# One unrolled pipeline in place of three passes, and a causal mask added by TensorE instead of a minimum on VectorE

## The chip, the cores and the metric

One core of one Trainium2 chip runs the whole kernel in one launch. The metric is the device time of the kernel in microseconds (us), and less is better. Engines are named as in the profile: PE is TensorE's matmul, PEld its weight load, DVE is VectorE, ACT is ScalarE, POOL is GpSimd, SP is SyncE, which here issues every transfer.

## What is computed

Sixteen images of 3x256x256 go through an edge filter, one block of attention with a causal mask, and one linear layer with the signs of a weight. All of it is in float32, S = D = 256, 16 heads of 16.

```python
gray = einsum('bchw,c->bhw', x, (0.2989, 0.587, 0.114))
h = abs(conv3x3(gray, scharr)).sum(axis=filters) / 2          # two 3x3 filters, zero padding
c_q, c_kv = norm(h) @ W_dq, norm(h) @ W_dkv                   # 256 -> 64 each
Q, K, V = c_q @ W_uq, c_kv @ W_uk, c_kv @ W_uv                # 64 -> 16 heads x 16
scores = where(tril, Q @ K.T / 4, -inf)
h = h + softmax(scores) @ V @ W_o
out = h + norm(h) @ sign(weight).T                            # norm is a layer norm without weights
```

## The kernel before

The kernel is written engine by engine: five programs, one for each engine, that wait for each other by semaphores. An engine runs its own program strictly in the written order, and an instruction that waits holds up all that stand behind it. There are 128 partitions, so an image of 256 rows lies in T = 2 tiles.

**Front pass.** SP loads an image (`x_sb`), ACT and DVE make it gray (L557, L686, L689), SP stores it with a border to DRAM (`gray_padded`) and loads it again as overlapping bands (`rows`, five transfers). PE applies the filters as products with `band` (L824), ACT takes absolute values (L563), DVE adds the two filters into `h_all`, forms mean and variance (`bn_stats`, `bn_aggr`) and the normalised `xn`. PE transposes it (L817), compresses to 64+64 (L853) and expands to queries, keys (L845) and values (L859). To reach float32 precision with bf16 products, each of query and key is cut into three bf16 parts: ACT casts the first (L573), DVE takes the rest (L724) and casts the second (L727), POOL takes the third (L503). SP stores the parts to DRAM (`qk_parts`) and later loads them in the layout in which six products of parts are one contraction of 96 rows (`q_st`, `k_st`, twelve transfers an image).

**Attention pass.** It starts when the front pass is through. Per image there are four groups g of four heads. For group g, PE forms the scores of the second half of the queries against all keys (`ps_hi`, L876 and mask L878) and of the first half against the first keys (`ps_lo`, L890 and mask L892). DVE takes their negated maxima (L752, L756). POOL cuts the maxima of two groups into three bf16 parts (`cut_max`, L515 to L523), PE transposes them, ACT copies them, SP moves them to three more rows of `q_st`. One iteration later PE forms the transposed scores of the same image with the maximum subtracted: first key block into `ps_k0` (L906, and the mask as a product of an identity with `mask_kq`, L908), second key block into `ps_k1` (L915, no mask product). DVE applies the mask of the second block, by a minimum of `ps_k1` with `cap_kq` (L761). ACT takes the exponentials (L600, L608), PE multiplies by the values with a column of ones (L927, L930), ACT copies (L616), PE transposes (L947), DVE divides (L733, L736), SP stores the result to DRAM (`attn_scratch`).

**Tail pass.** SP loads the attention output, PE transposes it (L817) and multiplies by `w_out` (L980), DVE adds `h_all` and normalises (L778, L790), PE transposes and multiplies by the signs `w_sign` (L980), DVE adds and SP stores.

What sets the order is written by hand: in each pass each engine has a step for "image n", and steps of neighbouring images are interleaved by constant offsets. The middle of each pass is a hardware loop (`Fori`) over pairs of images, the ends are unrolled. Buffers of one pass are used again in the next (`shared`, `parts`, `xn`), and the eight PSUM banks of 2 KB are laid out anew for each.

## Time and profile before

| | |
|---|---|
| three timed runs | 499.44, 499.70 and 503.98 us, median 499.70 us |
| the profiled execution | 499.42 us by the same clock, span of the trace 497.1 us |
| busy PE, PEld | 404.2 us (81%), 301.0 us (61%) |
| busy DVE, ACT, POOL | 357.1 us (72%), 223.2 us (45%), 94.1 us (19%) |
| instructions on PE, DVE, ACT, POOL | 3780 matmuls, 655, 404, 204 |
| DMA | 82.09 MB, mean 165 GB/s; the queue's packets took 58.3% of sixteen engines' span |
| mean granted clock of TensorE | 0.935 of full speed |

Busy time is counted from the first to the last instruction (the span); 2.3 us of the execution lie around it. A busy PE is one with a matmul under way, since matmuls overlap in the pipeline: the distance from one start to the next says what one costs PE, not its own length. A float32 product of 128x256 is recorded as two matmuls. The shares are means over three passes that differ, so the rows below are taken from the middle of each pass.

### The profile page before, as it was taken

What the parts mean: (1) busy time and instruction counts of PE and PEld (TensorE: products, weight loads), DVE (VectorE), ACT (ScalarE), POOL (GpSimd) and SP (SyncE); (2) the same over time, 40 slices, a digit from 0 to 9 for tenths busy, and PEclk for the clock granted to TensorE, in tenths of its full rate; (3) what the DMA queues carried; (4) which work ended last, traced back from release to release, by engine and by line L of the source; (5) the groups of instructions that cost most, each with busy time, mean ns of one, the idle gap of its engine ahead of it and who ended that gap; (6) DMA issues with size and microseconds to landing.
All of it is one profiled execution on the core that took longest, in us unless ns stands there. A gap on an engine that the chain in (4) does not pass through costs nothing.

```text
span 497.1 us, 11506 instructions
## 1 busy us (share of the span) xinstructions
PE 404.2 (81%) x3780; PEld 301.0 (61%) x3780; DVE 357.1 (72%) x655; ACT 223.2 (45%) x404; POOL 94.1 (19%) x204
## 2 busy tenths in 40 slices
PE   0068867678759667899999999999999987999995
PEld 0034634446536454567777777777777755787874
DVE  2765988877795436678888888888888835676664
ACT  2034535344444341366566656655566663222231
POOL 8500322322241133111111111111111100000000
PEclk9986978878898895799999999999999999999999
DMA  4999999999996955444444444444444222333231
GB/s 151 236 241 253 244 248 267 264 258 259 259 276 178 228 157 157 135 134 142 137 144 145 150 146 136 137 142 139 141 142 145 72 87 65 113 98 123 88 107 63
DMA packets 80863, 82.09 MB, mean 165 GB/s; under 512 B 6890, under 2 KB 74698, under 8 KB 80842
## 3 DMA queue, kind: packets, MB, share of 16 engines
q1 hardware_dynamic: 80842, 81.81, 58.3%
q8 instruction: 12, 0.20, 0.2%
q14 instruction: 9, 0.07, 0.0%
HBM read 56.17 MB, written 25.23 MB: 164 GB/s over the span
## 4 chain that ended last, share of the span: by engine, by line
PE 49%; DMA 23%; SPq 10%; issue 7%; ACT 5%; DVE 4%; POOL 1%; ACTq 0%; DVEq 0%; POOLq 0%
DMA gray_padded<-gray 16%; PE bank L980 11%; PE bank L876 6%; PE bank L906 5%; PE bank L927 5%; PE bank L947 4%; SPq L337 3%; SPq L359 3%; PE bank L908 3%; PE bank L890 3%; PE bank L878 3%; PE bank L892 3%; PE bank L915 2%; PE bank L930 2%; PE bank L817 2%
## 5 line engine op out<-in xcount | busy, mean ns | idle before, releaser
L752 DVE TENSOR_REDUCE neg_max<-bank 128x4 f32<-128x1024 f32 x64 | 78.3, 1223 | 26.5 <-PE bank L878 26.5
L600 ACT ACTIVATE shared<-bank 128x1024 f32<-128x1024 f32 x64 | 65.6, 1025 | 70.3 <-PE bank L908 70.3
L824 PE MATMUL bank<-shared,band 128*32 128x256 f32 x512 | 44.1, 503 | 37.3 <-DMA shared<-gray_padded 37.3
L503 POOL TENSOR_TENSOR parts<-rest,parts 128x1024 bf16<-128x1024 f32 x16 | 38.5, 2404 | 133.3 <-DVE parts L727 133.3
L876 PE MATMUL bank<-k_st,q_st 96*128 96x256 bf16 x256 | 48.7, 285 | 7.5 <-DMA k_st<-qk_parts 3.3
L824 PEld LDWEIGHTS bank<-shared,band 128*32 128x32 f32 x512 | 18.8, 134 | 57.6 <-issue 46.0
L761 DVE TENSOR_TENSOR bank<-bank,cap_kq 128x512 f32<-128x512 f32 x64 | 44.2, 691 | 4.3 <-PE bank L915 4.3
L906 PE MATMUL bank<-q_st,k_st 99*128 99x256 bf16 x256 | 46.3, 274 | 0.6 <-DMA q_st<-max_rows 0.6
L927 PE MATMUL bank<-shared,v_now 128*32 128x256 f32 x512 | 42.7, 389 | 1.2 <-ACT shared L616 1.2
L756 DVE TENSOR_REDUCE neg_max<-bank 128x4 f32<-128x512 f32 x64 | 43.6, 681 | 0.0
L563 ACT ACTIVATE edge<-bank 128x512 f32<-128x512 f32 x32 | 19.1, 598 | 54.0 <-PE bank L824 53.9
L608 ACT ACTIVATE shared<-bank 128x512 f32<-128x512 f32 x64 | 38.2, 597 | 10.7 <-DVE bank L761 10.4
L878 PE MATMUL bank<-mask_qk,ident_bf 128*128 128x256 bf16 x128 | 36.5, 285 | 0.0
L515 POOL CAST max_parts<-neg_max 128x16 bf16<-128x16 f32 x32 | 6.3, 196 | 158.1 <-DVE neg_max L756 158.1
L980 PE MATMUL bank<-w_sign,xn_t 128*128 128x256 f32 x128 | 31.9, 392 | 5.1 <-ACT xn_t L623 5.1
L908 PE MATMUL bank<-mask_kq,ident_bf 128*128 128x256 bf16 x128 | 35.2, 275 | 0.0
L876 PEld LDWEIGHTS bank<-k_st,q_st 96*128 96x128 bf16 x256 | 21.7, 100 | 21.0 <-issue 12.9
L980 PE MATMUL bank<-w_out,a_t 128*128 128x256 f32 x128 | 30.4, 381 | 1.4 <-ACT a_t L627 1.4
L695 DVE TENSOR_TENSOR h_all<-edge 128x256 f32 (+1 forms) x32 | 13.8, 439 | 24.5 <-ACT edge L563 24.5
L689 DVE SCALAR_TENSOR_TENSOR gray<-shared,gray 128x512 f32<-128x512 f32 x16 | 31.0, 1938 | 0.6
L906 PEld LDWEIGHTS bank<-q_st,k_st 99*128 99x128 bf16 x256 | 24.8, 99 | 10.6 <-issue 1.0
L980 PEld LDWEIGHTS bank<-w_sign,xn_t 128*128 128x128 f32 x128 | 23.0, 189 | 11.4 <-ACT xn_t L623 8.9
(100 smaller groups left out, 794.3 us busy)
## 6 DMA issues: line engine op xcount, KB each, us to landing
shared<-in_x SPq DMA_DIRECT2D x16, 768.0 KB, 7.0
shared<-gray_padded SPq DMA_DIRECT2D x48, 256.0 KB
qk_parts<-parts SPq DMA_DIRECT2D x16, 768.0 KB, 6.6
q_st<-qk_parts SPq DMA_DIRECT2D x96, 128.0 KB, 2.6
k_st<-qk_parts SPq DMA_DIRECT2D x96, 128.0 KB, 2.7
gray_padded<-gray SPq DMA_DIRECT2D x16, 258.0 KB, 6.3
attn_scratch<-attn SPq DMA_DIRECT2D x16, 256.0 KB, 2.5
a_sb<-attn_scratch SPq DMA_DIRECT2D x16, 256.0 KB, 2.8
```

The lines of the kernel that those rows point to most:

```text
L503: pool.tensor_tensor(parts[:, done.slot, SLOTS_OF_PART[2], :, :], rest[:, :, :, :], parts[:, done.slot, SLOTS_OF_PART[1], :, :], ALU.subtr ...
L600: nc.scalar.activation(probs[:, g, :, 0:S], ps_k0, ACT.Exp, scale=SCALE).then_inc(exp0_done, 1)
L752: nc.vector.tensor_reduce(neg_max[:, 1, heads], ps_hi, AX.X, ALU.max, negate=True).then_inc(max_hi_done, 1)
L756: nc.vector.tensor_reduce(neg_max[:, 0, heads], ps_lo, AX.X, ALU.max, negate=True).then_inc(max_lo_done, 1)
L761: nc.vector.tensor_tensor(ps_k1, ps_k1, cap_kq[:, :].unsqueeze(1).to_broadcast([P, G, P]), ALU.min).then_inc(capped, 1)
L824: last = nc.tensor.matmul(ps_edge[b * RB:(b + 1) * RB, t, f, :], band[:, f, :], rows[:, here.slot, t * (P // RB) + b, :], start=True, stop ...
L876: nc.tensor.matmul(ps_hi[:, b * two + i, :], q[:, hh, P:S], k[:, hh, :], start=(i == 0), stop=False, skip_group_check=True)
L878: last = nc.tensor.matmul(ps_hi[:, b * two:(b + 1) * two, P:S], ident_bf[:, :], mask_qk[:, 0:two, :], start=False, stop=True, skip_group_c ...
L906: nc.tensor.matmul(ps_k0[:, b * two + i, :], k[:, hh, 0:P], q[:, hh, :], start=(i == 0), stop=False, skip_group_check=True)
L908: last = nc.tensor.matmul(ps_k0[:, b * two:(b + 1) * two, 0:P], ident_bf[:, :], mask_kq[:, :, :], start=False, stop=True, skip_group_check ...
L927: nc.tensor.matmul(ps_o[i * VW:(i + 1) * VW, :], v_now[:, a.slot, 0, g * G + i, :], probs[:, g, i, 0:S], start=True, stop=False, skip_grou ...
L980: last = nc.tensor.matmul(dst[:, t, :], src_t[:, c, t * P:(t + 1) * P], w[:, c, :], start=(c == 0), stop=(c == T - 1))
```

## The change

The three passes become one. Each engine's program is a single loop over i = -6 to 20, unrolled by Python, in which every stage stands once with its own offset: image i+4 is made gray, i+3 is filtered, i+2 is normalised, compressed, expanded and cut into parts, i has its maxima taken, i-1 its key scores and half of its values, i-2 the other half, i-3 the projection, i-4 the last layer. With it:

- `attn_scratch` is gone: the attention output goes from SBUF straight to its transpose (16 stores and 16 loads of 256 KB less). `h_all` and `v_all` become rings of eight and five images, and POOL's copy of the values (L535) is gone, ACT copies into the ring.
- The normalisation moves from DVE and ACT (variance, square root on ACT, reciprocal, L715 and L790) to POOL (`normalize_x`, `normalize_y`): four operations on 128x2, with a power of -0.5 for the root, and two `tensor_scalar` of 128x256 each. The cast of the second part (L727) moves from DVE to ACT (`second_part`).
- The first part and its rest are taken in two halves. The absolute values are one ACT operation of 128x1024 in place of two of 512. `expand_qk` contracts 64 rows (queries from rows 0 to 63, keys from 64 to 127) where it contracted 128 rows, half of them zeros.
- PSUM banks are shared by stages that now run side by side: banks 0 and 1 by `ps_hi`, `ps_edge`, `ps_y`, `ps_z`; bank 2 by `ps_lo`, `ps_at`; 3 and 4 by `ps_k0`, `ps_qk`; 5 by `ps_k1`, `ps_mt`, `ps_yt`; 7 by `ps_xt`, `ps_c`, `ps_v`, `ps_ot`. The waits in the functions of PE say whose reader must be through.
- The mask of the second key block is one more product per group, identity by `mask_kq` (now four heads wide), added into `ps_k1`. The minimum L761 and its semaphore `capped` are gone, ACT waits for `k1_done`.

The core of the diff; the functions not shown hold the same operations as before, with the new waits:

```diff
+            for i in range(-4, LAST + 1):
+                if live(i + 1):
+                    store_parts(i + 1)
+                if live(i - 1):
+                    load_max_rows(i - 1, 1)
+                if live(i + 4):
+                    store_gray(i + 4)
+                if live(i + 6):
+                    load_x(i + 6)
+                if live(i - 4):
+                    store_z(i - 4)
+                if live(i + 1):
+                    load_operands(i + 1, 0)
+                if live(i):
+                    load_max_rows(i, 0)
+                if live(i + 4):
+                    load_rows(i + 4)
+                if live(i + 1):
+                    load_operands(i + 1, 1)
...
+            def normalize_x(n):
+                pool.wait_ge(mv_done, T * (n + 1))
+                pool.tensor_scalar(var[:, :], mv[:, :, 1], EPS, None, ALU.add).then_inc(var_done, 1)
+                pool.wait_ge(var_done, n + 1)
+                pool.tensor_tensor(rstd[:, :], var[:, :], power[:, :], ALU.pow).then_inc(rstd_done, 1)
+                pool.wait_ge(rstd_done, n + 1)
+                pool.tensor_tensor(shift[:, :], mv[:, :, 0], rstd[:, :], ALU.mult).then_inc(shift_done, 1)
+                pool.wait_ge(shift_done, 2 * n + 1)
+                pool.tensor_scalar(shift[:, :], shift[:, :], -1.0, None, ALU.mult).then_inc(shift_done, 1)
+                pool.wait_ge(shift_done, 2 * n + 2)
+                need(pool, xt_done, n)
+                for t in range(T):
+                    pool.tensor_scalar(xn[:, t, :], h_ring[:, n % H_RING, t, :], rstd[:, t:t + 1],
+                                       shift[:, t:t + 1], ALU.mult, ALU.add).then_inc(xn_done, 1)
...
+                pool.wait_ge(part1_done, n + 1)
...
+            for i in range(FIRST, LAST + 1):
+                if live(i - 1):
+                    cut_max(i - 1, 1)
+                if live(i + 2):
+                    normalize_x(i + 2)
+                if live(i - 3):
+                    normalize_y(i - 3)
+                if live(i):
+                    cut_max(i, 0)
+                if live(i + 2):
+                    third_part(i + 2)
...
+            def second_part(n):
+                act.wait_ge(rest_done, 2 * (n + 1))
+                nc.scalar.copy(parts[:, n % 2, SLOTS_OF_PART[1], :, :], rest[:, :, :, :]).then_inc(part1_done, 1)
...
+                    exp_second(i - 1, 3)
+                if live(i + 3):
+                    both_edges(i + 3)
+                if live(i - 1):
+                    copy_o(i - 1, 1)
+                if live(i + 2):
+                    second_part(i + 2)
+                if live(i - 3):
+                    copy_yt(i - 3)
...
-
-                        dve.wait_ge(k1_done, NG * done.n + g + 1)
-                        nc.vector.tensor_tensor(ps_k1, ps_k1,
-                                                cap_kq[:, :].unsqueeze(1).to_broadcast([P, G, P]),
-                                                ALU.min).then_inc(capped, 1)
...
+            nc.vector.memset(w_v[0:DC, :], 0.0)
+            for i in range(FIRST, LAST + 1):
+                if live(i):
+                    max_hi(i, 0)
+                    max_lo(i, 0)
+                if live(i - 4):
+                    add_z(i - 4)
+                if live(i + 4):
+                    rest_of_gray(i + 4)
...
-            steps(dve, tail, 0, 1)
+                if live(i):
+                    max_hi(i, 1)
+                    max_lo(i, 1)
+                if live(i - 3):
+                    add_y(i - 3)
+                if live(i):
+                    max_hi(i, 2)
+                    max_lo(i, 2)
+                if live(i - 2):
+                    normalize(i - 2, 0)
+                if live(i + 2):
+                    rest_of_parts(i + 2)
+                if live(i):
+                    max_hi(i, 3)
+                    max_lo(i, 3)
+                if live(i + 3):
+                    sum_edges(i + 3)
+                if live(i - 2):
...
+            def expand_qk(n):
+                pe.wait_ge(c_copied, n + 1)
+                need(pe, exp0_done, NG * upto(n - 4) + (3 if live(n - 3) else 0))
+                need(pe, rest_done, 2 * n)
+                for t in range(T):
+                    for i, low in ((0, 0), (1, DC)):
+                        last = nc.tensor.matmul(ps_qk[:, i, t, :],
+                                                w_qk[low:low + DC, t, :, :].rearrange("p d h -> p (d h)"),
+                                                c_t[low:low + DC, :], start=True, stop=True)
+                        if t == T - 1:
...
+            def key_scores_second(n, g):
+                q = q_st[0:KM, n % 2, :, :]
+                k = k_st[0:KM, n % 2, :, :]
...
+                if g == 1:
+                    need(pe, mt_copied, 2 * (n + 1))
+                if g == 3:
+                    need(pe, mt_copied, 2 * (n + 1) + (1 if live(n + 1) else 0))
                 for i in range(G):
                     hh = g * G + i
-                    last = nc.tensor.matmul(ps_k1[:, i, :], k[:, hh, P:S], q[:, hh, P:S],
-                                            start=True, stop=True)
...
+            def feed_forward(n):
+                pe.wait_ge(yt_copied, n + 1)
+                need(pe, max_hi_done, NG * upto(n + 3) + (1 if live(n + 4) else 0))
+                need(pe, abs_done, upto(n + 6))
+                need(pe, y_done, upto(n))
+                product(ps_z, yn_t, w_sign, ffn_done)
...
+                if live(i):
+                    hi_scores(i, 0)
+                    lo_scores(i, 0)
+                if live(i - 1):
+                    key_scores_first(i - 1, 0)
+                    key_scores_second(i - 1, 0)
+                if live(i - 4):
+                    feed_forward(i - 4)
+                if live(i - 2):
+                    values(i - 2, 2)
+                if live(i - 3):
...
+                if live(i + 2):
+                    turn_x(i + 2)
+                if live(i):
+                    hi_scores(i, 1)
+                    lo_scores(i, 1)
+                if live(i - 1):
+                    key_scores_first(i - 1, 1)
+                if live(i + 2):
+                    compress(i + 2)
+                if live(i - 1):
+                    key_scores_second(i - 1, 1)
+                if live(i - 3):
+                    project(i - 3)
+                if live(i - 2):
+                    values(i - 2, 3)
+                if live(i):
+                    hi_scores(i, 2)
+                    lo_scores(i, 2)
+                if live(i - 1):
+                    key_scores_first(i - 1, 2)
+                if live(i - 2):
+                    turn_output(i - 2, 0)
+                if live(i - 1):
+                    key_scores_second(i - 1, 2)
+                    values(i - 1, 0)
+                if live(i + 2):
+                    expand_qk(i + 2)
+                if live(i):
+                    turn_max(i, 0)
+                if live(i):
+                    hi_scores(i, 3)
+                    lo_scores(i, 3)
+                if live(i + 2):
+                    expand_v(i + 2)
+                if live(i - 1):
+                    key_scores_first(i - 1, 3)
+                    key_scores_second(i - 1, 3)
+                if live(i + 3):
+                    filters(i + 3)
+                if live(i - 1):
+                    values(i - 1, 1)
+                if live(i - 2):
+                    turn_output(i - 2, 1)
+                if live(i - 3):
+                    turn_y(i - 3)
```

PE, the end of an iteration. Before, group 3 of the attention pass: key scores of `ps_k0` and `ps_k1`, transposes of the output (`shared` is the tile of unnormalised output there), products of probabilities and values:

```order
L906 MATMUL bank<-q_st,k_st 128x256 x2
L908 MATMUL bank<-mask_kq,ident_bf 128x2x128
L906 MATMUL bank<-q_st,k_st 128x256 x2
L908 MATMUL bank<-mask_kq,ident_bf 128x2x128
L915 MATMUL bank<-q_st,k_st 128x128 x4
L947 MATMUL bank<-ident,shared 128x128 x4
L927 MATMUL bank<-shared,v_now 32x256 x4
L930 MATMUL bank<-shared,v_now 32x128 x4
```

The same place of the changed program, from the key scores of group 3 to the last instruction of the iteration:

```order
L849 MATMUL bank<-q_st,k_st 128x256 x2
L851 MATMUL bank<-mask_kq,ident_bf 128x2x128
L849 MATMUL bank<-q_st,k_st 128x256 x2
L851 MATMUL bank<-mask_kq,ident_bf 128x2x128
L868 MATMUL bank<-q_st,k_st 128x128 x4
L870 MATMUL bank<-mask_kq,ident_bf 128x512
L766 MATMUL bank<-rows,band 32x256 x16
L880 MATMUL bank<-probs,v_ring 32x256 x4
L883 MATMUL bank<-probs,v_ring 32x128 x4
L909 MATMUL bank<-ident,o_un 128x128 x4
L746 MATMUL bank<-ident,yn 128x128 x4
```

The mask product of the second block (L870) is new, and between the key scores and the values now stand the filters of image i+3 (L766); the iteration ends with the transposes of `o_un` and `yn`.

PE, the head of an iteration. Before, the key scores of group 0 up to the values:

```order
L906 MATMUL bank<-q_st,k_st 128x256 x2
L908 MATMUL bank<-mask_kq,ident_bf 128x2x128
L906 MATMUL bank<-q_st,k_st 128x256 x2
L908 MATMUL bank<-mask_kq,ident_bf 128x2x128
L915 MATMUL bank<-q_st,k_st 128x128 x4
L940 MATMUL bank<-ident_bf,max_parts 24x128 x2
L927 MATMUL bank<-shared,v_now 32x256 x4
L930 MATMUL bank<-shared,v_now 32x128 x4
```

Changed, from the key scores of group 0 on:

```order
L849 MATMUL bank<-q_st,k_st 128x256 x2
L851 MATMUL bank<-mask_kq,ident_bf 128x2x128
L849 MATMUL bank<-q_st,k_st 128x256 x2
L851 MATMUL bank<-mask_kq,ident_bf 128x2x128
L868 MATMUL bank<-q_st,k_st 128x128 x4
L870 MATMUL bank<-mask_kq,ident_bf 128x512
L753 MATMUL bank<-w_sign,yn_t 128x256 x4
L880 MATMUL bank<-probs,v_ring 32x256 x4
L883 MATMUL bank<-probs,v_ring 32x128 x4
L746 MATMUL bank<-ident,attn 128x128 x4
L896 MATMUL bank<-ident_bf,max_parts 24x128 x2
L746 MATMUL bank<-ident,xn 128x128 x4
```

The product with the signs for image i-4 (L753), which writes the bank that `ps_hi` of this very group has filled, now stands ahead of the values, and the transposes of `attn` (i-3) and `xn` (i+2) around the transposes of the maxima.

POOL, from one cut of the maxima on. Before, in the attention pass:

```order
L515 CAST max_parts<-neg_max 128x2x8
L517 TENSOR_TENSOR max_rest<-neg_max,max_parts 128x16
L521 CAST max_parts<-max_rest 128x2x8
L523 TENSOR_TENSOR max_parts<-max_rest,max_parts 128x2x8
L515 CAST max_parts<-neg_max 128x2x8
L517 TENSOR_TENSOR max_rest<-neg_max,max_parts 128x16
L521 CAST max_parts<-max_rest 128x2x8
L523 TENSOR_TENSOR max_parts<-max_rest,max_parts 128x2x8
L535 COPY v_now<-v_all 128x16x16 x2
```

Changed, from the third part of image i+2 at the end of one iteration into the next:

```order
L457 TENSOR_TENSOR parts<-rest,parts 128x1024
L415 CAST max_parts<-neg_max 128x2x8
L417 TENSOR_TENSOR max_rest<-neg_max,max_parts 128x16
L420 CAST max_parts<-max_rest 128x2x8
L422 TENSOR_TENSOR max_parts<-max_rest,max_parts 128x2x8
L427 TENSOR_SCALAR var<-mv 128x2
L429 TENSOR_TENSOR rstd<-var,power 128x2
L431 TENSOR_TENSOR shift<-mv,rstd 128x2
L433 TENSOR_SCALAR shift<-shift 128x2
L437 TENSOR_SCALAR xn<-h_ring,rstd,shift 128x256 x2
L442 TENSOR_SCALAR var<-mv 128x2
```

Behind the third part stand the cut of the maxima and then the six operations of `normalize_x`, whose result the transposes of `xn` wait for.

## Rows read from the trace of the kernel before

**Rows 1.** Stretch of front, attention, tail: length, busy PE, PEld, DVE, ACT, POOL, PEclk, DMA, GB/s
```profile
75.58:154.23 78.65, 57.18 (x404) 39.13 (x404) 60.85 (x107) 33.45 (x61) 20.36 (x8) 0.83 0.96 256
...
230.74:387.22 156.48, 152.40 (x1922) 117.27 (x1921) 130.76 (x193) 96.22 (x169) 28.27 (x120) 1.00 0.47 143
415.00:488.00 73.00, 67.44 (x353) 56.59 (x351) 50.95 (x151) 20.54 (x46) 0.00 (x0) 1.00 0.32 101
```

**Rows 2.** Timeline of PE, one attention iteration, full clock
```profile
302.52 0.38 PE L876 MATMUL bank<-k_st,q_st 96*128 96x256 bf16 x2
...
303.41 0.38 PE L892 MATMUL bank<-mask_qk,ident_bf 128*128 128x512 bf16 x1
303.63 0.38 PE L906 MATMUL bank<-q_st,k_st 99*128 99x256 bf16 x2
...
304.52 0.61 PE L947 MATMUL bank<-ident,shared 128*128 128x128 f32 x4
305.06 0.64 PE L927 MATMUL bank<-shared,v_now 128*32 128x256 f32 x8
...
305.85 0.39 PE L876 MATMUL bank<-k_st,q_st 96*128 96x256 bf16 x2
...
315.07 0.66 PE L947 MATMUL bank<-ident,shared 128*128 128x128 f32 x4 [0.35 <-ACT max_rows L591]
315.56 0.38 PE L876 MATMUL bank<-k_st,q_st 96*128 96x256 bf16 x2
```

**Rows 3.** Timeline of PE, front pass: first filters, then an image at full clock
```profile
26.90 3.64 PE L824 MATMUL bank<-shared,band 128*32 128x256 f32 x32
...
49.43 1.93 PE L824 MATMUL bank<-shared,band 128*32 128x256 f32 x32 [0.36 <-DMA shared<-gray_padded]
51.29 0.65 PE L817 MATMUL bank<-ident,xn 128*128 128x128 f32 x4
51.78 1.03 PE L845 MATMUL bank<-c_t,w_q 128*128 128x256 f32 x4
...
53.51 1.03 PE L853 MATMUL bank<-xn_t,w_c 128*128 128x256 f32 x4
```

**Rows 4.** Chain that ended last, tail pass, two images (start, length)
```profile
473.45 3.72 PE bank L980 x16
478.29 3.72 PE bank L980 x16
```

**Rows 5.** Groups by line and form: DVE and ACT work that the change keeps, moves or removes
```profile
L752 DVE TENSOR_REDUCE neg_max<-bank 128x4 f32<-128x1024 f32 x64 | 78.3, 1223 | 26.5 <-PE bank L878 26.5
L600 ACT ACTIVATE shared<-bank 128x1024 f32<-128x1024 f32 x64 | 65.6, 1025 | 70.3 <-PE bank L908 70.3
...
L761 DVE TENSOR_TENSOR bank<-bank,cap_kq 128x512 f32<-128x512 f32 x64 | 44.2, 691 | 4.3 <-PE bank L915 4.3
...
L736 DVE TENSOR_TENSOR attn<-bank,recip 128x256 f32<-128x256 f32 x32 | 13.6, 425 | 2.2
...
L778 DVE BATCH_NORM_STATS2 stats<-parts 128x6 f32<-128x256 f32 x32 | 12.0, 419 | 2.4 <-DVE parts L772 1.7
```

**Rows 6.** Groups by line and form: POOL, and two DVE operations of one form
```profile
L503 POOL TENSOR_TENSOR parts<-rest,parts 128x1024 bf16<-128x1024 f32 x16 | 38.5, 2404 | 133.3 <-DVE parts L727 133.3
...
L689 DVE SCALAR_TENSOR_TENSOR gray<-shared,gray 128x512 f32<-128x512 f32 x16 | 31.0, 1938 | 0.6
...
L686 DVE SCALAR_TENSOR_TENSOR gray<-shared,gray 128x512 f32<-128x512 f32 x16 | 11.0, 688 | 7.3 <-ACT gray L557 7.3
...
L535 POOL COPY v_now<-v_all 128x256 f32 x24 | 8.9, 398 | 0.0
```

**Rows 7.** Timeline of POOL, the first and the last of one cut of the maxima
```profile
305.42 0.20 POOL L515 CAST max_parts<-neg_max 128x16 bf16<-128x16 f32 x1 [4.79 <-DVE neg_max L756]
...
306.36 0.22 POOL L523 TENSOR_TENSOR max_parts<-max_rest,max_parts 128x16 bf16<-128x16 f32 x1
```

**Rows 8.** Timeline of PE, first scores of image 0
```profile
188.29 0.58 PE L876 MATMUL bank<-k_st,q_st 96*128 96x256 bf16 x2 [2.86 <-DVE rest L724]
```

1044 lines of the change are left out of this document (445 added, 599 removed).

## The prediction

> **What bounds the kernel now.** I read the busy time by stretch first, since the page's shares are means over three passes with different limits [rows 1]. The front pass takes about 10 us an image and is bound by transfers: DMA share 0.96 at 256 GB/s, while PE is under work for 57 of 79 us at a mean granted clock of 0.83. The attention pass is bound by PE: 152.4 of 156.5 us busy, clock 1.00, DMA share only 0.47. The tail is bound by PE too, 67.4 of 73.0 us, DMA share 0.32. So the question is whether one pipeline can lay the front's transfers under the PE work of the other two, and what it costs in new waits. The first scores stand at 188.29 [rows 8]: by then only the front pass is behind, 38% of the time, and PE, the engine with most work, was mostly waiting for rows from DRAM.
>
> Next come the timelines of PE, for its price list at full clock. Since matmuls overlap, I take the distance between starts.
>
> **The change, part by part. PE's work for one image.**
> - Attention: 315.56 - 302.52 = 13.04 us less the one idle gap of 0.35 = 12.69 [rows 2]. That is exactly one image in steady state.
> - New mask of the second block: the product of the same form, L892, takes 303.63 - 303.41 = 0.22 [rows 2]; four groups, 0.88.
> - Front: filters 51.29 - 49.43 = 1.86, a transpose of a tile pair 0.49, queries and keys 53.51 - 51.78 = 1.73, so 0.87 each for compression and values [rows 3]. Sum 5.82.
> - Tail: the period is 478.29 - 473.45 = 4.84 with 3.72 from first to last end of its two products [rows 4]; as they have the form of the queries' and keys' products, I count 2 x 1.73 + 2 x 0.49 = 4.44.
>
> Together 23.83 us an image, 381 us for sixteen. This is the floor; before, the passes take 10 + 13.0 + 4.8 = 27.9.
>
> **The other engines.** The minimum that goes saved DVE 44.2 us in all (691 ns, four an image) [rows 5]. In a loop with 24 us of PE work DVE has per image 4 x 1.9 for the maxima and some 8.5 for everything else, 16 to 17 us; with the minimum it would have 19. It isn't the bound either way, so the mask by itself is a bad trade in steady state (14 us more on the bound engine); it gains where PE waits for DVE. The scratch transfers that vanish are 8.4 of 82 MB; the 74 MB left over some 415 us of loop are 178 GB/s, against the 256 that the front pass reached [rows 1]. I take the transfers as hidden: rows and images are issued an iteration ahead, operands half an iteration. If that cover fails, each late load costs PE directly.
>
> **The waits in a steady iteration.** The weak place is the seam. Let E be the end of image i+3's filters. PE goes on with values (305.85 - 305.06 = 0.79 [rows 2]), two transposes (0.54 and 0.49), scores and key scores of group 0 (2.00 + 0.22): it reaches the sign product at E + 4.05. That product writes bank 0, which DVE must have read. DVE before it: ACT's absolute values (1.02, form of L600), the sum 0.69 (form of L761), two `bn_stats` 0.84, two aggregates at some 0.4, the division with its reciprocal 0.7, then the maximum 1.22 [rows 5]: E + 5.0 with the hops. PE waits **1.0 us**.
>
> The second strand at the seam is POOL's. Behind the absolute values ACT copies an output (0.37) and casts the second part (1.02), to E + 2.5; POOL takes the third part (2.40 with DVE in its way [rows 6], 2.1 without), cuts the maxima (306.58 - 305.42 = 1.16 [rows 7]), and normalises image i+2. No row shows a `tensor_scalar` or a power on POOL. From below: four small operations at the pace of the cut, 0.31 each, 1.25, and two at the price of the POOL copy of 128x256, 0.40 each [rows 6]: 2.05, so `xn` is ready at E + 8.0. From above: the two at L503's rate per element, 0.6 each, and 1 us more for the power, 3.5 us. PE comes for it at E + 5.0 + 1.73 + 0.79 + 0.49 + 0.1 = E + 8.1. I take the lower end, as one-input copies are the nearer row; then both strands tie, and anything POOL takes beyond that passes to the period one for one. The Trainium skill speaks against this part of the change: its GPSIMD Engine Reference, section 4.1, gives elementwise work to VectorE and calls GPSIMD about half as fast for two inputs. The rows agree for two inputs (2404 ns for 1024 elements against DVE's 691 for 512), not for the copy, 398 ns; by the page's factor the two scalings would take 0.8 each and the period would be 0.8 us longer.
>
> A third, small one: scores of group 2 wait for the sum `y` in the same bank, 0.69 + 0.2 against the values' 0.79, so 0.1 to 0.2. DVE's gray operations can be held by POOL (L689 takes 1938 ns beside L503 where L686, the same form, takes 688 [rows 6]); here they have about 1 us of slack before the group 1 maxima matter. Steady period: 23.83 + 1.0 + 0.2 = **25.0 us**.
>
> **Filling and draining.** Filters of image 0 started at 26.90 [rows 3]; they end at about 28. While filling, one image follows another only as fast as the chain filters, absolute values, second part, third part, normalisation, transpose, compression, expansion, next filters: 1.0 + 1.0 + 2.4 + 2.0 + 0.5 + 0.6 + 0.9 + 0.4 + 1.7 + 0.9 + 1.9 and hops, 14.3 us; the sign weights stand in the first round, 3 us. So filters of 1 end at 45, of 2 at 59, and the parts of image 0, out at 48, stored and loaded, let the first scores start at **60 us** (before 188.29). Iterations 0 to 3 are partly empty of PE work but pay the POOL strand: 16, 23, 24, 25 us, to 148. Iterations 4 to 12 are full: 9 x 25.0 = 225, to 373. Iterations 13 to 15 lack filters, then the whole front: 23 + 19.5 + 19.5, to 435. The drain (16 to 19) has 13, 8, 5 and 2 us of PE work and longer and longer chains through POOL's normalisation: 14 + 10 + 9.5 + 5.5 = 39. Span **474 us**; with the 2.3 us around the span **476 us**, to be held against 499.4 for the profiled execution and 499.7 for the median, so they compare directly.
>
> **The rivals.**
> - *Row groups side by side.* `expand_qk` now contracts 64 rows, queries on the lower and keys on the upper half. What it would do: the two run at once, 0.87 instead of 1.73 for 14 images in the loop, 12 us: 464. For it: four 32-column products at once are in the trace (filters, 32 matmuls in 1.86 us where eight of the 128-column form take 1.73 [rows 3]). Against: no row shows row halves, and turning over the maxima right behind it waits for POOL, which would eat some. The Trainium skill, TensorEngine Tiling, sections Theoretical Speedup and Key Properties, has such a pair up to 2x faster and a drain on each change of mode. Chance 0.20, 456 to 468.
> - *POOL's strand becomes the bound (slower).* Place: `normalize_x` between the maxima's cut and the transposes of `xn`. The lower price ties with PE; at 3.5 us instead of 2.05, 1.45 us more an image, 16 images and the four rounds of filling: 476 + 29 = 505. It decides from about 1.2 us over the lower price. For: a power and scalars from pointers have no row. Against: small POOL operations all take 0.2 us. Chance 0.12, 495 to 512.
> - *Transfers come late.* SP issues some 20 transfers an iteration in fixed order and waits for each condition in turn; the maximum rows and operands stand behind stores of 768 KB. 1 us an iteration: 492. Against: DMA share would be about 0.7. Chance 0.08, 486 to 500.
> - *Leaner.* The seam's wait is absorbed, filling takes 50: 476 - 16 - 10 = 450. Chance 0.13, 444 to 456.
> - The change does less than it says if the stages don't overlap at all: 27.9 + 0.9 an image, 0.02, over 500.
>
> **How the numbers follow.** The forecast has 0.45, with 462 to 490 as its own range. Leaving out the tail of the leaner case and the top of POOL's, the range is 448 to 502. A measurement here tells about 1% (5 us) from no change: faster by more is all up to 494.7, 0.82; within, 0.08; slower 0.10.
>
> **What would show it.** In the trace after: periods of 25 us between the same L892-like product of successive images; PE busy over 93% in the middle at clock 1.00; a wait of about 1 us on DVE's maximum ahead of the sign product; the transposes of `xn` with little wait; first scores near 60; no DVE work on `ps_k1`. I'm wrong if the largest wait of PE in the middle is for `xn` (POOL), for `q_st` or `rows` (DMA), or if the period is below 24 (row groups), or if filling takes over 75 us.

## The result

The changed kernel is slower: 516.11 us median (514.06 to 517.54, four runs) against 499.57 us, ratio 1.031 with a 95% interval of 1.025 to 1.037. The profiled execution has a span of 514.0 us, 16.9 us more than before. From its page, the span, the busy times, TensorE's granted clock and the DMA share in forty slices:

```profile
span 514.0 us, 10154 instructions
...
PE 405.8 (79%) x3784; PEld 288.3 (56%) x3844; DVE 247.8 (48%) x444; ACT 227.8 (44%) x385; POOL 164.3 (32%) x361
...
PEclk9975568798979999999999999999999999999987
DMA  5953877765664757575757575737372425300000
```

PE has as much work as before (405.8 against 404.2 us), DVE 109 us less, POOL 70 us more. The digits of the clock are low at the left, as before over the whole front pass, and once more in the last slices.

The same view by stretches as in [rows 1] (length, busy PE, PEld, DVE, ACT, POOL, clock, DMA share, GB/s): from the start to the first scores, iteration 0, the steady middle, and the drain from iteration 16 on:

```profile
0.00:68.72 68.72, 25.32 (x141) 13.73 (x142) 18.04 (x35) 12.98 (x20) 22.88 (x38) 0.75 0.68 176
68.72:89.11 20.39, 12.94 (x97) 9.18 (x100) 11.32 (x18) 5.35 (x10) 5.77 (x11) 0.75 0.68 177
...
167.00:402.00 235.00, 213.09 (x2136) 154.59 (x2164) 134.24 (x241) 126.57 (x216) 84.80 (x189) 1.00 0.60 162
...
466.60:514.00 47.40, 33.00 (x238) 22.88 (x237) 10.86 (x28) 12.53 (x22) 7.38 (x18) 0.89 0.07 23
```

In the middle 213.1 of 235 us are busy, 91%, where the attention pass of before had 97% [rows 1]; the clock is 1.00 and the DMA share 0.60. Up to the first scores PE is busy for 25.3 of 68.7 us at a mean granted clock of 0.75, in the drain for 33.0 of 47.4 us at 0.89.

**Period.** PE's timeline of one steady iteration (start, length), which starts at 272.96 with the scores of group 0:

```profile
265.82 0.28 PE L896 MATMUL bank<-ident_bf,max_parts 128*24 128x128 bf16 x2 [0.16 <-POOL max_parts L422]
...
267.24 1.13 PE L799 MATMUL bank<-w_v,c_t 64*128 64x256 f32 x4
268.30 0.39 PE L849 MATMUL bank<-q_st,k_st 99*128 99x256 bf16 x2
...
274.95 0.38 PE L870 MATMUL bank<-mask_kq,ident_bf 128*128 128x512 bf16 x1
276.10 1.97 PE L753 MATMUL bank<-w_sign,yn_t 128*128 128x256 f32 x8 [0.76 <-issue]
...
279.37 0.28 PE L896 MATMUL bank<-ident_bf,max_parts 128*24 128x128 bf16 x2
280.83 0.66 PE L746 MATMUL bank<-ident,xn 128*128 128x128 f32 x4 [1.19 <-POOL xn L437]
...
290.69 1.13 PE L789 MATMUL bank<-c_t,w_qk 64*128 64x256 f32 x8
291.99 0.28 PE L896 MATMUL bank<-ident_bf,max_parts 128*24 128x128 bf16 x2 [0.16 <-POOL max_parts L422]
```

The period is 291.99 - 265.82, the same product one iteration apart, = 26.17 us; over seven iterations the starts of the filters are 26.18 apart. Four waits can be read. The sign product starts at 276.10 where the mask product ahead of it (L870) has taken its 0.22 by 275.17, so 0.93; the profile names no releaser (`issue`), but this product needs the bank that DVE's maximum of group 0 reads, and that ends at 274.78 + 1.21 = 275.99. The transposes of `xn` wait 1.19 for POOL, those of the maxima 0.16, and about 0.15 is lost ahead of group 2. That leaves 23.7 us of PE's work. The row of `expand_qk` (L789) is 1.13 long, and its distance to the next start is 1.30 with the wait of 0.16 in it; in iteration 0, where nothing waits, it is 1.06. The same work took 1.73 from start to start [rows 3]: the two row halves do run side by side. The values' expansion, also 64 rows, costs 268.30 - 267.24 = 1.06 instead of 0.87. So an iteration gains 0.43 in one place and gives back 0.19 in the next.

**The strand that PE waits for.** POOL in the same iteration, with the scalings of `yn` for comparison:

```profile
273.82 2.13 POOL L457 TENSOR_TENSOR parts<-rest,parts 128x1024 bf16<-128x1024 f32 x1 [8.05 <-ACT parts L505]
275.89 0.19 POOL L415 CAST max_parts<-neg_max 128x16 bf16<-128x16 f32 x1
...
277.03 0.23 POOL L427 TENSOR_SCALAR var<-mv 128x2 f32<-128x2 f32 x1
277.33 0.72 POOL L429 TENSOR_TENSOR rstd<-var,power 128x2 f32<-128x2 f32 x1
...
278.76 2.02 POOL L437 TENSOR_SCALAR xn<-h_ring,rstd,shift 128x256 f32<-128x256 f32 x2
...
289.83 1.10 POOL L452 TENSOR_SCALAR yn<-y,rstd,shift 128x256 f32<-128x256 f32 x2
```

Behind the third part (2.13) and the cut (1.14), the normalisation of `xn` takes from 277.03 to 280.78, 3.75 us: the power alone 0.72, and the two scalings 2.02, where the two of `yn`, the same form, take 1.10. DVE's timeline suggests why; its maximum of group 0, and its two gray operations:

```profile
274.78 1.21 DVE L663 TENSOR_REDUCE neg_max<-bank 128x4 f32<-128x1024 f32 x1
...
278.71 0.68 DVE L632 SCALAR_TENSOR_TENSOR gray<-x_sb,gray 128x512 f32<-128x512 f32 x1
279.42 0.93 DVE L635 SCALAR_TENSOR_TENSOR gray<-x_sb,gray 128x512 f32<-128x512 f32 x1
```

The gray operations, each with two inputs in SBUF, lie inside POOL's scalings, and the second takes 0.93 where the first takes 0.68: the two engines hold each other up, as L503 and L689 did [rows 6], and POOL's share of that is 2.02 - 1.10 = 0.9 us. A run below tests it. The Trainium skill has the rule: SBUF — State Buffer, section "SBUF: two separate sides", says that a VectorE operation with two SBUF inputs and a GpSimd operation that reads SBUF take turns at a shared pair of ports, each for its whole instruction. The trace agrees: 2.02 against 1.10.

**The ends.** PE while filling; L766 are the filters of images 0, 1 and 2, L780 a compression:

```profile
25.81 3.64 PE L766 MATMUL bank<-rows,band 102*32 102x256 f32 x32 [25.81 <-DMA rows<-gray_padded]
...
38.08 2.07 PE L780 MATMUL bank<-xn_t,w_c 128*128 128x256 f32 x4 [0.67 <-ACT xn_t L490]
...
44.33 3.64 PE L766 MATMUL bank<-rows,band 102*32 102x256 f32 x32
...
63.94 3.54 PE L766 MATMUL bank<-rows,band 102*32 102x256 f32 x32
```

A filling round takes 18.5 and 19.6 us. The filters take 3.64 us in it, at full clock 1.86 [rows 3], the compression 2.07 instead of 1.03. The clock granted to PE is 0.50 from 35 to 65 us. The first scores start at 68.72. At the other end the clock falls again twice, behind a row of short waits (0.49 to 1.23 us) and behind a single one of 4.68 us:

```profile
493.58 3.50 PE L753 MATMUL bank<-w_sign,yn_t 128*128 128x256 f32 x8 [0.67 <-ACT yn_t L545]
...
505.05 1.12 PE L746 MATMUL bank<-ident,yn 128*128 128x128 f32 x4 [4.68 <-POOL yn L452]
506.84 3.78 PE L753 MATMUL bank<-w_sign,yn_t 128*128 128x256 f32 x8 [0.67 <-ACT yn_t L545]
```

The same product of eight matmuls takes 3.50 and 3.78 us here and 1.97 in the middle; between the two, at 498.37, the projection of the same form is back at 1.99.

### The profile page after: what moved, and what is told of

Same layout as the page of the kernel before. It is cut to its first block, busy times and chain, and to the rows that moved or that the text cites. A ratio compares the mean times of both kernels' runs of the same rounds, so it can differ in the third digit from the quotient of the medians.

```text
span 514.0 us, 10154 instructions
## 1 busy us (share of the span) xinstructions
PE 405.8 (79%) x3784; PEld 288.3 (56%) x3844; DVE 247.8 (48%) x444; ACT 227.8 (44%) x385; POOL 164.3 (32%) x361
## 4 chain that ended last, share of the span: by engine, by line
PE 25%; POOL 22%; issue 22%; DVE 5%; ACT 1%; POOLq 0%
PE bank L753 8%; POOL parts L457 5%; POOL xn L437 4%; PE bank L746 3%; POOL yn L452 3%; PE bank L849 2%; DVE y L686 2%; POOL rstd L444 2%; PE bank L780 2%; PE bank L818 2%; POOL rstd L429 2%; DVE stats L690 1%; POOL max_parts L422 1%; PE bank L880 1%; POOL max_rest L417 1%
## 5 line engine op out<-in xcount | busy, mean ns | idle before, releaser
L524 ACT ACTIVATE probs<-bank 128x1024 f32<-128x1024 f32 x64 | 65.5, 1023 | 64.4 <-PE bank L851 64.1
L766 PE MATMUL bank<-rows,band 102*32 102x256 f32 x512 | 36.0, 428 | 26.9 <-DMA rows<-gray_padded 25.8
L535 ACT COPY o_un<-bank 128x256 f32<-128x256 f32 x64 | 23.8, 372 | 60.6 <-PE bank L883 60.6
L655 DVE TENSOR_TENSOR rest<-bank,parts 128x512 f32<-128x512 f32 x32 | 20.6, 686 | 46.5 <-ACT parts L501 46.5
L753 PE MATMUL bank<-w_sign,yn_t 128*128 128x256 f32 x128 | 34.7, 419 | 9.8 <-issue 7.7
L880 PE MATMUL bank<-probs,v_ring 128*32 128x256 f32 x512 | 40.6, 389 | 0.9
L766 PEld LDWEIGHTS bank<-rows,band 102*32 102x32 f32 x512 | 16.7, 120 | 42.0 <-issue 35.4
L529 ACT ACTIVATE probs<-bank 128x512 f32<-128x512 f32 x64 | 38.0, 593 | 0.3
L753 PEld LDWEIGHTS bank<-w_sign,yn_t 128*128 128x128 f32 x128 | 25.0, 205 | 17.3 <-issue 11.2
L485 ACT ACTIVATE edge<-bank 128x1024 f32<-128x1024 f32 x16 | 16.4, 1024 | 39.1 <-PE bank L766 39.1
L753 PE MATMUL bank<-w_out,a_t 128*128 128x256 f32 x128 | 30.5, 381 | 1.4 <-ACT a_t L540 1.3
```

The source lines that it names most:

```text
L524: nc.scalar.activation(probs[:, g, :, 0:S], ps_k0, ACT.Exp, scale=SCALE).then_inc(exp0_done, 1)
L529: nc.scalar.activation(probs[:, g, :, S:S + P], ps_k1, ACT.Exp, scale=SCALE).then_inc(exp1_done, 1)
L753: last = nc.tensor.matmul(dst[:, t, :], src_t[:, c, t * P:(t + 1) * P], w[:, c, :], start=(c == 0), stop=(c == T - 1))
L766: last = nc.tensor.matmul(ps_edge[b * RB:(b + 1) * RB, t, f, :], band[0:KC, f, :], rows[0:KC, n % 2, t * (P // RB) + b, :], start=True, st ...
L880: nc.tensor.matmul(ps_o[i * VW:(i + 1) * VW, :], v_ring[:, n % V_RING, 0, g * G + i, :], probs[:, g, i, 0:S], start=True, stop=False, skip ...
```

## The experiments

Periods are the mean distance between starts of the filters in the steady middle. The changed kernel has 26.18 and 516.1 us.

**The mask alone, from both sides.** First the changed kernel with the minimum on DVE again:

```diff
-                nc.tensor.matmul(ps_k1[:, :, :], ident_bf[:, :], mask_kq[:, :, :], start=False, stop=True,
-                                 skip_group_check=True).then_inc(k1_done, 1)
...
+            def cap(n, g):                      # on DVE, behind max_lo(i, g)
+                dve.wait_ge(k1_done, NG * n + g + 1)
+                nc.vector.tensor_tensor(ps_k1, ps_k1, cap_kq[:, :].unsqueeze(1).to_broadcast([P, G, P]),
+                                        ALU.min).then_inc(capped, 1)
```

> The changed kernel with the mask of the second key block by a minimum on VectorE again, as before; everything else as changed. Theory (POOL's strand at the seam and PE at its lower clock in filling and draining set the time): the mask product costs PE 0.22 us in each of four groups, but in group 0 the time saved only becomes waiting, since between the filters and the transposes of xn the strand through ACT and POOL decides; the period falls by 0.66 from 26.17 to 25.5 us, the time by some 10 us to 506. Rival A (PE's work alone decides): 0.88 an image, 14 us, 502. Rival B (the mask product relieves a VectorE that holds PE up): the time rises by 5 us or more.

Measured: period 25.80. The four runs took 503.6, 510.1, 512.7 and 513.3 us, all below the changed kernel's 514.1 to 517.5, but too far apart to size a difference of some us; the profiled one has a span 3.3 us below. PE in the middle:

```profile
263.74 0.28 PE L913 MATMUL bank<-ident_bf,max_parts 128*24 128x128 bf16 x2 [0.38 <-POOL max_parts L427]
...
273.80 1.96 PE L771 MATMUL bank<-w_sign,yn_t 128*128 128x256 f32 x8 [0.98 <-issue]
```

The direction is right, rival B is out, but the mask is worth 0.38 a period and not 0.66: the idle time ahead of the sign product grew from 0.76 to 0.98, that for the cut of the maxima from 0.16 to 0.38. A DVE that has the minimum to do is late with its maxima.

Then the kernel before with the mask product and nothing else:

```diff
-                        nc.vector.tensor_tensor(ps_k1, ps_k1,
-                                                cap_kq[:, :].unsqueeze(1).to_broadcast([P, G, P]),
-                                                ALU.min).then_inc(capped, 1)
+                nc.tensor.matmul(ps_k1[:, :, :], ident_bf[:, :], mask_kq[:, :, :], start=False, stop=True,
+                                 skip_group_check=True).then_inc(k1_done, 1)
```

> The kernel before with nothing changed but the mask of the second key block added by TensorE and the minimum taken out. Its attention pass is bound by PE, so all theories that count PE's work say 4 x 0.22 = 0.88 us an image, period 13.04 to 13.9, time 499.6 to 513. If the minimum was what held up the exponentials and through them PE, the time stays within 3 us of before or falls.

Measured: 509.3 us, ratio to before 1.018 (1.012 to 1.025). PE's transposes of the output, one attention iteration apart:

```profile
266.33 0.66 PE L942 MATMUL bank<-ident,shared 128*128 128x128 f32 x4
...
280.02 0.66 PE L942 MATMUL bank<-ident,shared 128*128 128x128 f32 x4
```

The attention period is 280.02 - 266.33 = 13.69, 0.65 more than before [rows 2]; sixteen times that is 10.4 us, as is the difference of the spans (507.5 and 497.1). The idle gap of 0.35 ahead of these transposes [rows 2] is gone, and the rest of the 0.88, 0.23, was covered by it. So the mask product alone costs the kernel before 10 us. In the pipeline it costs 0.38 x 16 = 6 us by the periods, of the 16.5 lost.

**POOL's strand.** The two scalings of `xn` on DVE:

```diff
+            def scale_x(n):                     # on DVE, behind add_z; POOL keeps rstd and shift
+                dve.wait_ge(shift_done, 2 * n + 2)
...
+                for t in range(T):
+                    nc.vector.tensor_scalar(xn[:, t, :], h_ring[:, n % H_RING, t, :], rstd[:, t:t + 1],
+                                            shift[:, t:t + 1], ALU.mult, ALU.add).then_inc(xn_done, 1)
```

> The changed kernel with the two scalings that make xn (128x256 each) on VectorE in place of POOL; the power and the other small operations stay on POOL. Theory (POOL's strand): in the trace xn comes 1.25 us after PE is ready for it, of which 0.9 because POOL's two scalings take 2.02 us beside VectorE's gray operations, where the scalings of yn take 1.10. On VectorE they take 0.8 and are done when PE arrives: period 26.17 to 25.0, and 1 us less in each filling round; 16 x 1.15 + 3, the time falls by 20 us to 496. Rival A (PE's own work and changes of mode): no change. Rival C (transfers late): no change.

Measured: 496.7 us, period 24.92. The only wait of PE that the view lists for the middle (in total, how often, the longest; L758 is the sign product of this version):

```profile
PE bank L758 <- issue: 7.0, 9, 0.9
```

The wait for `xn` isn't there any more, that ahead of the sign product stands alone. This one move takes 19 us off, 16 x 1.26 = 20 by the periods, and brings the time just below that of before (0.993, 0.990 to 0.997).

How much of it was contention, without moving POOL's work:

```diff
-                if live(i + 4):
+                if live(i + 4) and not live(i):
                     rest_of_gray(i + 4)
...
                 if live(i):
                     max_hi(i, 1)
                     max_lo(i, 1)
+                if live(i + 4) and live(i):
+                    rest_of_gray(i + 4)         # stood behind the maxima of group 0
```

> The changed kernel; VectorE's two gray operations of image i+4 stand behind the maxima of group 1 instead of those of group 0, so that they no longer run beside POOL's scalings of xn. Theory (POOL's strand, part of it contention): the pair of scalings falls from 2.02 to 1.10 us, PE's wait for xn from 1.25 to 0.33, period 26.17 to 25.25, the time by 12 us to 504. Rival (POOL's scalings of xn are slow by themselves, their input being a ring of eight images): period and time unchanged.

Measured: 502.5 us, period 25.26. POOL's scalings, and PE's wait for them:

```profile
266.20 1.10 POOL L437 TENSOR_SCALAR xn<-h_ring,rstd,shift 128x256 f32<-128x256 f32 x2
```
```profile
267.35 0.66 PE L748 MATMUL bank<-ident,xn 128*128 128x128 f32 x4 [0.27 <-POOL xn L437]
```

1.10 instead of 2.02, and 0.27 instead of 1.19 of waiting. The Trainium skill, GPSIMD Engine Reference, section 4.1, calls GPSIMD about line rate for one input. The runs differ for this form: alone a scaling takes 555 ns (L452, mean of 32) for the 256 elements that a copy takes in 398 [rows 6]. The factor that the prediction worked with is the section's for two inputs, and a scaling has one. The contention is shown: the same instructions in another place of DVE's program.

Not all of the 13.6 us is the edit's, though. Up to iteration 0 this program is that of the changed kernel, yet the profiled execution fills faster: the filters of image 1

```profile
43.13 1.93 PE L768 MATMUL bank<-rows,band 102*32 102x256 f32 x32
```

take 1.93 and not 3.64 us, the rounds 17.8 and 17.0 instead of 18.5 and 19.6, and the first scores come 38.0 us behind the first filters instead of 42.9. At which level PE works while it fills differs between executions of one program. I read the level from the lengths here: the granted clock is recorded as 1.00 from 30 to 45 us, though the compression in it takes 2.07.

And without touching any operation, POOL's order (SP's store of the parts moves behind the load of the maximum rows with it):

```diff
                 if live(i + 2):
                     normalize_x(i + 2)
+                if live(i + 1):
+                    third_part(i + 1)
                 if live(i - 3):
                     normalize_y(i - 3)
                 if live(i):
                     cut_max(i, 0)
-                if live(i + 2):
-                    third_part(i + 2)
```

> The changed kernel with POOL's program in another order: the third part of an image is taken behind the normalisation of the next instead of ahead of the cut of the maxima (and SP stores it behind the load of the maximum rows). No operation is added or left out. Theory (what makes PE wait for xn is what stands ahead of it on POOL): xn is ready 1.5 us before PE comes, the wait of 1.25 is gone, period 24.9; in filling, the parts of image 0 come about 4 us later; the time falls by 16 - 4 = 12 us to 504. Rival (the power and the scalings themselves are too slow wherever they stand): a wait for xn stays, the time is unchanged or higher by the 4 us.

Measured: 489.3 us, ratio to before 0.981 (0.979 to 0.983), period 24.96. The normalisation and the third part now:

```profile
276.40 0.23 POOL L427 TENSOR_SCALAR var<-mv 128x2 f32<-128x2 f32 x1 [3.87 <-DVE mv L649]
...
278.15 1.09 POOL L437 TENSOR_SCALAR xn<-h_ring,rstd,shift 128x256 f32<-128x256 f32 x2
279.21 2.14 POOL L457 TENSOR_TENSOR parts<-rest,parts 128x1024 bf16<-128x1024 f32 x1
```

No wait for `xn` is left in the middle; POOL now waits for the variance instead. The gain beyond the expected 12 us lies ahead of the steady middle, where I had expected a loss. Of the 28.6 us between the two spans, 10.2 are from the filters of image 6 to those of image 15, 13.3 from image 3 to image 6 (65.6 instead of 78.9 us, with 1.4 us of waiting for `xn` in it instead of 9.7), and 4.8 from image 0 to image 3. These filling rounds take 17.7 and 16.5 us instead of 18.5 and 19.6. In the second the third part had stood ahead of the normalisation: in the changed kernel that starts at 52.29, 1.4 us after its variance is there. The rest of the 4.8 can't be put down to the order: the filters of image 1 take 1.93 us here, and the run before had such rounds without the new order. The chain I had written down in the prediction and not drawn the conclusion.

**The clock at the ends.** Extra matmuls without a reader where PE idles:

```diff
+            def warm(bank_no, count):
+                for _ in range(count):
+                    nc.tensor.matmul(bank[:, bank_no, :], ident_bf[:, :],
+                                     mask_qk[:, :, :].rearrange("p g s -> p (g s)"), start=True, stop=True)
+            warm(6, 56)                         # ahead of the first filters; 22, 26, 16 ahead of turn_x,
                                                # 18 ahead of turn_y in iterations 17 and 18
```

> The changed kernel with extra matmuls that nothing reads, on PE alone, where PE idles: 56 before the first filters, 22, 26 and 16 before the transposes of xn of images 0, 1 and 2, and 18 before each of the transposes of yn in iterations 17 and 18. Theory (filling is slow because PE's work in it runs at the lower clock): filters 3.64 to 1.9, compression and expansion from 2.07 to 1.0 each, so a filling round 19.5 to about 14.5, first scores from 68.7 to about 57, and 3 us in the drain; the time falls by 15 us to 501. Rival (the length of the chain through ACT, VectorE and POOL decides, the clock is incidental): within 3 us.

Measured: 504.7 us, 11.5 us less, period unchanged at 26.18. The filters of images 0, 1, 2 and a compression:

```profile
24.87 3.64 PE L766 MATMUL bank<-rows,band 102*32 102x256 f32 x32 [3.79 <-DMA rows<-gray_padded]
...
38.39 1.13 PE L780 MATMUL bank<-xn_t,w_c 128*128 128x256 f32 x4 [0.67 <-ACT xn_t L490]
...
41.91 1.93 PE L766 MATMUL bank<-rows,band 102*32 102x256 f32 x32
...
56.63 1.93 PE L766 MATMUL bank<-rows,band 102*32 102x256 f32 x32
```

The rounds take 17.0 and 14.7 us. The compression is back at 1.13, the filters at 1.93 from the second on, and the first scores start at 61.04. PE's work at the lower level, not the length of the chain through the other engines, made filling longer than forecast. What the extra matmuls gain depends on the level that an execution would have been granted without them.

**Two waits at one seam.** The sign product behind the values, alone:

```diff
-                if live(i - 4):
-                    feed_forward(i - 4)
                 if live(i - 2):
                     values(i - 2, 2)
+                if live(i - 4):
+                    feed_forward(i - 4)
```

> The changed kernel with PE's product with the signs behind the values of group 2 instead of ahead of them. Theory (two strands tie at the seam and POOL's ends last): the wait of 0.93 us for VectorE's maximum ahead of the sign product shrinks to about 0.1, but the wait for xn grows by the same 0.8; period 26.17 and time 516 unchanged within 2 us. Rival (each wait counts for itself): period 25.3, time 505.

Measured: 525.9 us, 10 us more; both theories missed it. PE and then POOL:

```profile
279.47 1.96 PE L753 MATMUL bank<-w_sign,yn_t 128*128 128x256 f32 x8
...
284.21 1.12 PE L746 MATMUL bank<-ident,xn 128*128 128x128 f32 x4 [2.13 <-POOL xn L437]
285.11 0.64 PE L818 MATMUL bank<-k_st,q_st 96*128 96x256 bf16 x2
...
312.06 0.66 PE L746 MATMUL bank<-ident,xn 128*128 128x128 f32 x4 [2.04 <-POOL xn L437]
```
```profile
282.15 2.00 POOL L437 TENSOR_SCALAR xn<-h_ring,rstd,shift 128x256 f32<-128x256 f32 x2
```

The waits do merge as expected: the sign product follows without one, the transposes of `xn` wait 2.13, which is 1.19 + 0.93. But behind this one longer wait the matmuls then run at the lower level, the transposes 1.12 instead of 0.66, the scores 0.64 for two instead of 0.38, until 3.5 to 4 us later. Not each time: of eight such waits in the middle (2.04 to 2.13 us) six are followed by it, and those periods are 27.7 to 27.9 us; two aren't, as at 312.06, and there the period stays 26.2. The granted clock of the middle is 0.96 instead of 1.00, the period 27.34 in the mean. One wait of 2.1 us costs more here than two that add up to it.

The same swap with the scalings on DVE:

> The kernel with the scalings of xn on VectorE (496.7 us, period 24.90) and in addition the sign product behind the values. Theory: with POOL's strand short, the wait for VectorE's maximum is the last one at the seam, and the swap that is worth nothing alone now takes 0.8 us out of the period: 24.1, 16 x 0.8 = 13 us, 484. Rival (each wait counts for itself, so also alone): the same here, but then also in the run before. Rival (the scalings on VectorE then become the next wait): 492 or more.

Measured: 496.6 us, period 24.84: nothing gained, the second rival. PE:

```profile
264.21 1.97 PE L758 MATMUL bank<-w_sign,yn_t 128*128 128x256 f32 x8
...
267.60 0.66 PE L751 MATMUL bank<-ident,xn 128*128 128x128 f32 x4 [0.78 <-DVE xn L651]
```

The sign product starts without a wait, and 0.78 us of waiting have moved to `xn`, now for DVE. Counted from the end of the filters, `xn` is ready at 8.2 us with and without the swap, and the sign product and `add_z` stand where they stood, as the values now fill what was a wait. Only PE comes 0.86 us sooner. Two strands hold `xn` there and end together: `scale_x` starts as `add_z` ends, and 0.04 us behind POOL's last small operation. The run doesn't say which alone would be enough.

With POOL's order instead, where `xn` is ready 5.9 us behind the filters and needs nothing of the sign product:

> The kernel with POOL's third part behind the normalisation (489.3 us, period 24.93) and in addition the sign product behind the values. Theory (waits at the seam are strands that end at the same place; each is worth something only when the other is short): xn was ready 2 us before PE came for it, so here the swap, which lost 10 us alone, takes the 0.9 us wait for VectorE's maximum out of the period: 24.1, time 477. Rival (a matmul order that puts values first costs by itself): 489 or more.

Measured: 479.5 us, ratio 0.960 (0.953 to 0.967), period 24.02; 477 and 24.1 were expected. The swap that lost 10 us alone gains 10 here.

**All of it together**, once with the minimum on DVE, once with the mask product (POOL order, swap, extra matmuls 56, 18, 24, 8 and 18):

> POOL order, swap, the minimum on VectorE instead of the mask product, and the extra matmuls that keep PE's clock up in filling and draining. Theory: with no wait left at the seam, PE's work alone sets the period, and only here does the mask product cost its full 4 x 0.22: period 24.1 - 0.9 = 23.2; filling and draining 10 us less: 477 - 14 - 10 = 453, below both kernels by 9%. Rival (the minimum delays VectorE's maxima and gives back what PE saves): period 24 or more, 465.

> As the run before, but with the mask product on TensorE as in the changed kernel: POOL order, swap, extra matmuls. Theory: period 24.1, 467; the difference to the run before, 14 us, is the price of the mask product when nothing covers it (against 0.37 a period in the changed kernel as it is). Rival: no difference between the two.

Measured: 470.3 us with the minimum, ratio 0.940 (0.933 to 0.947), period 23.62; 475.2 us with the mask product, ratio 0.952 (0.945 to 0.959), period 24.02. The version with the minimum is the fastest. Its middle, with the waits that are left, and below them the one that the version with the mask product has there:

```profile
165.00:350.00 185.00, 179.60 (x1844) 132.43 (x1841) 136.40 (x238) 109.86 (x189) 66.48 (x161) 1.00 0.69 183
```
```profile
270.35 1.97 PE L771 MATMUL bank<-w_sign,yn_t 128*128 128x256 f32 x8 [0.20 <-issue]
...
283.90 0.28 PE L913 MATMUL bank<-ident_bf,max_parts 128*24 128x128 bf16 x2 [0.39 <-POOL max_parts L427]
```
```profile
284.02 0.28 PE L896 MATMUL bank<-ident_bf,max_parts 128*24 128x128 bf16 x2 [0.17 <-POOL max_parts L422]
```

PE is busy for 97% at clock 1.00. Both times were expected lower, 453 and 467. The mask's price is 0.40 a period and 5 us, not 14: the minimum shows up in the waits for DVE's maximum (0.20) and for the cut that follows from it (0.39 against 0.17 with the mask product). And the extra matmuls gain only 4 us on top of the POOL order and the swap (479.5 to 475.2). Their counts were guessed: the filters of image 2 still took 3.64 us, and the first scores came at 65.5, behind a wait of 5.1 us for the loads of `k_st` (64.0 and 4.5 with the mask product).

## Why the prediction was wrong

It said 476 us, faster, and the time is 516. The mechanism of the gain was as described: the transfers vanish under PE's work (share 0.60, no wait of PE for them in the middle), PE's work an image is 23.7 us against 23.83 from the rows (0.24 of it saved by the row halves, which the sum left out), the period is below the 27.9 of the three passes, and DVE isn't the bound. The error is in the prices around it. Against the span of 474, 514.0 is 40 us more:

| stretch | forecast | measured | more |
|---|---|---|---|
| to the first scores | 60 | 68.7 | 8.7 |
| iterations 0 to 3 | 88 | 98.9 | 10.9 |
| iterations 4 to 12 | 9 x 25.0 | 9 x 26.17 | 10.5 |
| iterations 13 to 15 | 62 | 63.5 | 1.5 |
| drain | 39 | 47.4 | 8.4 |

- **The step that failed first: the price of POOL's normalisation, taken at its lower bound.** 2.05 us was my value, 3.5 my upper bound, 3.75 the measurement. The power takes 0.72 and not 0.31, the scalings 0.55 each and not 0.40, and 0.9 us is contention with DVE's gray operations. I had seen that contention, but priced only DVE's side of it, as slack; the side that costs is POOL's, which was on the strand that ties. The rival "POOL's strand becomes the bound" had 505 with 3.5 us for this term, and it is what happened in the middle: a wait for `xn` of 1.2 us, and a period 1.17 longer than the 25.0 of the forecast. The wait is gone where the scalings are moved or POOL is reordered, and down to 0.27 where the gray operations are moved; the period falls to 24.92, 24.96 and 25.26.
- **The step that failed second: full-clock prices for filling and draining.** The chain of a round, 14.3 us, is right: with PE kept busy it is 14.7, and the first one 17.0 as forecast. But in the changed kernel PE, busy for 25 of 69 us up to the first scores, was granted half of its clock from 35 to 65 us, and its 5 us of work in a round became 10. The rows had it: the first filters at 3.64 and the front pass at a clock of 0.83 [rows 1, 3], and I used 3.64 for image 0 alone. That is most of the first row of the table: with the extra matmuls the first scores start at 61.0, against 60 forecast. Iterations 0 to 3 hold both errors: from the filters of image 3 to those of image 6 the clock is 0.89, and PE waits 9.7 us for `xn`. The drain does too: 3.5 and 3.8 us for sign products of 2.0, and a normalisation of 2.8 us on POOL in the last round.
- These two don't cover all of the 40 us. The spans of the runs fall by 28.6 us with POOL's order and by 4.1 more for the extra matmuls (475.1 to 471.0 with the swap in both), which would leave 481 of 514, an estimate, against 474. Of the drain no run took more than 3.4 us: what made it longer than the forecast's 39 stays open in the main.
- The wait for DVE's maximum ahead of the sign product was forecast at 1.0 and is 0.93, that ahead of group 2 at 0.1 to 0.2 and is 0.15. Both right. The wait of 0.16 for the maxima's cut wasn't in the sum.
- The row halves run side by side, the mechanism of that rival, but it said 0.87 us an image and the gain is 0.43 less 0.19 in the next product. "Leaner" isn't seen, and no late transfer in the middle; with the rest mended, the first scores waited for `k_st` (1.4 to 5.1 us in six of the runs).
- Chances: I gave 0.12 to the POOL case and let it end at 512. It and the clock at the ends add up, and the prediction had taken both near their cheap end.
- Not a matter of the pipeline: some 6 us of the 16.5 lost are the mask product, by the periods.

Why it is slower than before, then, in two numbers: sixteen periods of 26.2 instead of 27.9 save 27 us, while the ends, what the span has beyond these periods, grew from 51 us (497.1 - 446) to 95 (514.0 - 419). The three short passes together spend less on their beginnings and ends than the one long pipeline does. What of these 95 us is the length of the pipeline and what the two errors above wasn't measured apart; with POOL's order alone it is 86 (485.4 - 16 x 24.96), with the extra matmuls alone 85 (503.4 - 16 x 26.18).

## What to carry to other kernels

Where an operation moves to a slower engine, price the whole strand that ends in it, with what stands ahead of it in that engine's program and what runs beside it, and take the upper bound if the strand ties: reordering POOL's program alone took 27 us off here. Price the filling and draining of a long pipeline at the lengths that the trace shows for an engine that waits, not at those of the busy middle. And of several waits that end at one seam none can be valued by removing it alone: the same swap lost 10 us, gained nothing, or gained 10, depending on when the other strands ended.

## What the runs showed of the hardware

- Waits of PE of 2.04 to 2.13 us were followed by 3.5 to 4 us of matmuls at the lower level in six of eight iterations; waits of 1.19 and 0.93 in one iteration were not followed by any in the middle. One and the same filling program had its second filters at 3.64 us in one execution and at 1.93 in another.
- A `tensor_scalar` of 128x256 float32 on POOL takes 555 ns, a power of 128x2 takes 0.72 us (first ones 1.13), other operations on 128x2 about 0.2. Two scalings beside DVE operations with two SBUF inputs took 2.02 instead of 1.10 us.
- Products of 64 rows on the lower and upper half took less than one behind the other: eight matmuls of 256 columns in 1.06 us from start to start, 1.73 for the same on full rows.
